# Edge batch norm sums moved to TensorE, degree counts moved to the second edge stage

## The reference

```python
h = jnp.maximum(_layernorm(x), 0.0)
messages = jnp.concatenate([h[src], edge_rep[dst]], axis=-1)
messages = _bn_relu(messages @ W1, g1, b1)      # mean and variance over all 50000 edges
edge_new = segment_sum(messages, dst)
aggregate = segment_sum(edge_new[dst], src)
h = (1.0 + epsilon) * h + aggregate             # then two dense layers with batch norm
```

## Time and profile before

| | us |
|---|---|
| Median of 3 runs | 3554.77 (3550.27 to 3555.87) |
| Profiled execution, first to last instruction | 3565.2 |
| PE busy | 2424.9 (68%) |
| DVE busy | 2395.4 (67%) |
| POOL busy | 1734.6 (49%) |
| ACT busy | 1352.5 (38%) |

### The profile page before, as it was taken

How to read it: one execution, slowest core, us unless ns; L and a number is a source line. 1 busy time by engine, 2 the same in 40 slices (tenths; PEclk the granted TensorE clock), 3 DMA queues, 4 the chain that set the end, 5 groups by cost and what they waited for, 6 DMA issues and landing times. The chain is left out here.

```text
span 3565.2 us, 41686 instructions
## 1 busy us (share of the span) xinstructions
PE 2424.9 (68%) x12339; PEld 1976.6 (55%) x12339; DVE 2395.4 (67%) x4693; ACT 1352.5 (38%) x2800; POOL 1734.6 (49%) x1269
## 2 busy tenths in 40 slices
PE   4668733454555543666621999879999999925998
PEld 3522213454444443444421897469888988923788
DVE  5979945777777778877886544344565566615788
ACT  2268833444444441000000435424434434423776
POOL 0257887776667667888888777730000000042000
PEclk9779865555555555888855999889999999966999
DMA  9993224665555656555533774146545645340355
GB/s 373 351 355 34 22 26 130 174 171 164 165 165 166 172 170 137 133 142 134 143 40 39 202 177 89 1 103 185 175 126 172 185 130 173 118 103 8 109 173 176
DMA packets 338453, 517.84 MB, mean 145 GB/s; under 512 B 145379, under 2 KB 227100, under 8 KB 331580
## 3 DMA queue, kind: packets, MB, share of 16 engines
q1 hardware_dynamic: 190254, 436.41, 38.2%
q0 software_dynamic: 134768, 58.41, 14.2%
q10 hardware_dynamic: 13214, 20.35, 1.7%
HBM read 369.65 MB, written 145.38 MB: 144 GB/s over the span
## 5 line engine op out<-in xcount | busy, mean ns | idle before, releaser
L1133 PE MATMUL banks<-rows_r,lhs_r 128*128 128x448 f32 x3500 | 899.1, 372 | 84.0 <-issue 41.6
L728 POOL DMA_INDIRECT counts<-wts x391 | 637.4, 1630 | 307.9 <-DMA counts<-ring 141.0
L1133 PEld LDWEIGHTS banks<-rows_r,lhs_r 128*128 128x128 f32 x3500 | 667.8, 191 | 152.9 <-issue 74.8
L741 POOL DMA_INDIRECT weights<-wts x391 | 620.9, 1588 | 161.8 <-issue 159.1
L1133 PE MATMUL banks<-ring_r,lhs_r 128*128 128x448 f32 x1750 | 525.8, 370 | 0.0
L749 POOL DMA_INDIRECT reg<-tab_p,w x416 | 406.9, 978 | 217.9 <-issue 122.8
L548 DVE SCALAR_TENSOR_TENSOR ring_r<-ring,dinv,rows_r 128x896 fp32r<-128x896 f32 (+1 forms) x300 | 303.7, 1033 | 309.5 <-ACT rows_r L535 309.3
L1221 PE MATMUL banks<-lhs_r,oT 128*128 x416 | 203.3, 489 | 429.8 <-issue 346.6
L535 ACT ACTIVATE rows_r<-ring,dinv 128x896 fp32r<-128x896 f32 (+1 forms) x300 | 285.0, 951 | 399.3 <-PE banks L1133 342.0
L799 POOL DMA_INDIRECT el<-tab_l,base_i x25 | 24.0, 958 | 796.8 <-DMA tab_l<-reg 789.5
L1221 PEld LDWEIGHTS banks<-lhs_r,oT 128*128 128x128 f32 x416 | 131.9, 317 | 447.3 <-issue 447.0
(11 more groups left out here) (269 smaller groups left out, 4104.6 us busy)
## 6 DMA issues: line engine op xcount, KB each, us to landing
ring<-weights SPq DMA_DIRECT2D x225, 448.0 KB
ring<-counts SPq DMA_DIRECT2D x150, 448.0 KB
zbuf<-reg SPq DMA_DIRECT2D x208, 256.0 KB
reg<-zbuf SPq DMA_DIRECT2D x52, 1024.0 KB
counts<-ring SPq DMA_DIRECT2D x25, 1568.0 KB, 16.4
weights<-ring SPq DMA_DIRECT2D x25, 1568.0 KB
ring<-weights SPq DMA_DIRECT2D x75, 224.0 KB
dr<-low_rows_d SPq DMA_DIRECT2D x52, 256.0 KB
```

The costliest lines, as they stand in the source:

```text
L728: pool.indirect_dma_start(counts, bass.IndirectOffsetOnAxis(ap=ix_c[:, k:k + 1], axis=0), vals_c[:, k:k + 1], None, compute_op=ALU.add).th ...
L741: pool.indirect_dma_start(weights, bass.IndirectOffsetOnAxis(ap=ix_w[:, k:k + 1], axis=0), vals_w[:, k:k + 1], None, compute_op=ALU.add).t ...
L1133: m = pe.matmul(bank[:, 0:BLK], lhs[part], rows[:, c:c + BLK], start=first, stop=last)
```

## The change

ScalarE's squares and VectorE's running sum are gone. TensorE multiplies z with itself: for each chunk and each half of the channels, 128 columns of z against the same 128 columns and two columns of ones beside them. The diagonal of the result is the sum of squares, the ones' column the sum of z. So z lies with gaps between its rows (`ZW`), and the statistics are columns, one channel per partition, instead of rows. The degrees move from the first edge stage to the second, the clearing of `en` from VectorE to ScalarE. Eight tile numbers are loaded by one instruction. GpSimd issues one count after every eighth gather instead of every fourth, and fewer weights between the counts that follow.

```diff
-C_PER = 1
-W_FROM, W_PER, W_MID = 42, 7, (7, 7, 4, 3, 7)
+C_EVERY = 8
+W_FROM, W_PER, W_MID = 42, 7, (4,) * 15 + (3,)
...
+        def load_tiles(eng, regs, i):
+
+            eng.load(regs, tile_ix[0:1, 8 * i:8 * i + 8])
+            return [eng.snap(r, min_val=0, max_val=NT - 1) for r in regs]
...
                 for q in (2 * s, 2 * s + 1):
                     sp.dma_start(zbuf[:, 2 * q:2 * q + 2, :],
-                                 zz[q % ZS].rearrange("p (a c) -> p a c", c=H)).then_inc(z_stored[s % (ZS // 2)], 16)
+                                 z_rows(q)).then_inc(z_stored[s % (ZS // 2)], 16)
...
             for i in range(NPASS):
-                if i == 2:
-                    sp.wait_ge(stat_done, 1)
+                if i == 0:
+                    sp.wait_ge(z_acc, KQ)
...
                 gather(k)
-                if k % 4 == 3:
-                    add_counts(C_PER)
+                if k % C_EVERY == C_EVERY - 1:
+                    add_counts(1)
...
-            for i in range(NPASS):
-                for q in range(4 * i, 4 * i + 4):
-                    act.wait_ge(z_ready, q + 1)
-                    act.activation(zsq[q % SQ], zz[q % ZS], ACT.Square).then_inc(sq_ready, 1)
-                    for c in (2 * q, 2 * q + 1) if i < NBAT else ():
...
+            act.activation(bn_c[:, 3, :], bn_c[:, 2, :], ACT.Sqrt).then_inc(bn_std, 1)
+            for at_t in (en, en_odd):
+                act.activation(at_t, zeros[:, 0:H].unsqueeze(1).to_broadcast([P, NT, H]), ACT.Copy).then_inc(en_cleared, 1)
+            for c in range(NCH):
+                act.activation(dist[c % 2], cols[:, :], ACT.Abs, bias=t_nlo[:, c:c + 1]).then_inc(dist_ready, 1)
...
-                    tiles[2 * q:2 * q + 8] = [pe.value_load(tile_ix[0:1, k:k + 1], min_val=0, max_val=NT - 1) for k in range(2 * q, 2 * q + 8)]
+                    tiles[2 * q:2 * q + 8] = load_tiles(pe, pe_regs, q // 4)
...
+            def square_sums(q):
+
+                pe.wait_ge(z_ready, q + 1)
+                for k in range(2):
+                    for j in range(JH):
+                        o = 2 + k * (H + 2) + j * P
+                        a = o - 2 if j == 0 else o
+                        m = pe.matmul(stat_bank[j][:, 0:P + 2], zz[q % ZS][:, o:o + P], zz[q % ZS][:, a:a + P + 2],
+                                      start=(q == 0 and k == 0), stop=(q == KQ - 1 and k == 1))
+                m.then_inc(z_acc, 1)
...
                     add_q(q)
-                    if i and i <= NBAT:
-                        degrees(2 * q - 8)
-                        degrees(2 * q - 7)
+                    if q >= 2:
+                        square_sums(q - 2)
...
                     m.then_inc(m_sum, 1)
+                    if i < NBAT:
+                        degrees(2 * q)
+                        degrees(2 * q + 1)
...
-                if i < NBAT:
-                    degree_rows(i)
                 for q in range(4 * i, 4 * i + 4):
                     add_z(q)
-                    if q >= 2:
-                        sum_z(q - 2)
...
+                if i + 1 < NBAT:
+                    degree_rows(i + 1)
+                tiles = load_tiles(v, v_regs, i)
```

More of the change, by code:

```diff
@@ L290, in gnn_kernel, with z_rows @@
         low_sb = typed("low_sb", reg_at + 4 * at, 4 * P, BF16); at += 2 * P
[L291 removed]
+        low_sb_end = at
+        assert low_sb_end <= F0 + 44 * H
         gp = view(F0, 8, H)
[L294 to L305 removed]
+        Z_AT = F0 + 16 * H
+        zz = [view(Z_AT + k * ZW, ZW) for k in range(ZS)]
+        def z_rows(q):
+            return view(Z_AT + q % ZS * ZW + 2, 2, H + 2)[:, :, 0:H]
+        at = Z_AT + ZS * ZW
+        dr = [typed(f"dr{k}", reg_at + 4 * at + 2 * k * 8 * P, 8 * P, BF16) for k in range(2)]
+        at += 8 * P
+        oT = [rounded(f"oT{k}", at + k * 8 * P, 8 * P) for k in range(2)]
+        at += 2 * 8 * P
+        assert at <= 6 * W_ - NG * P
         at = F0 + 44 * H
@@ L1210, in _ @@
             tiles = [None] * KS
+            pe_regs = [pe.alloc_register(f"pe_tile{k}") for k in range(8)]
             def add_q(q):
@@ L1243, in _ @@
                     group_totals(TESTED[q])
-            pe.wait_ge(z_acc, KQ + 1)
-            for part in range(2):
-                for k in range(2):
-                    o = (2 * part + k) * H
-                    m = pe.matmul(stat_bank[:, part * H:(part + 1) * H], ones[:, :], zsum[:, o:o + H], start=(k == 0), stop=(k == 1))
-            m.then_inc(stat_done, 1)
-            pe.wait_ge(abs_a, 1)
+            pe.wait_ge(nb_ready, 1)
             for j in range(JH):
-                m = pe.transpose(ps[5][:, j * P:(j + 1) * P], absg[:, j * P:(j + 1) * P], ident[:, :])
-            m.then_inc(a_cols, 1)
+                m = pe.matmul(nb_ps[:, j * P:(j + 1) * P], bn_c[:, 7, j:j + 1].to_broadcast([P, P]), ident[:, :], start=True, stop=True)
+            m.then_inc(nb_rows, 1)
             for i in range(NPASS):
@@ L1662, in _ @@
-            v.wait_ge(a_cols, 1)
-            do(v.tensor_scalar(neg_a[:, :], ps[5][:, 0:H].rearrange("p (j c) -> p j c", j=JH)[:, :, 0], -1.0, None, ALU.mult))
+            v.wait_ge(z_acc, KQ)
+            mean_c, sq_c, var_c, std_c, a_c, ra_c, bt_c, nb_c = (bn_c[:, k, :] for k in range(8))
+            for j in range(JH):
+                o = 2 if j == 0 else 0
+                v.tensor_tensor(diag_t[:, j, :], stat_bank[j][:, o:o + P], ident[:, :], ALU.mult)
+                last = v.tensor_scalar(mean_c[:, j:j + 1], stat_bank[j][:, 0:1] if j == 0 else stat_bank[j][:, P:P + 1], 1.0 / E, None, ALU.mult)
@@ new lines, in _ @@
+            do(last)
+            do(v.tensor_reduce(sq_c, diag_t, AX_X, ALU.add))
+            do(v.tensor_tensor(var_c, mean_c, mean_c, ALU.mult))
+            do(v.scalar_tensor_tensor(var_c, sq_c, 1.0 / E, var_c, ALU.mult, ALU.subtract))
+            do(max_zero(var_c))
+            v.tensor_scalar(var_c, var_c, BN_EPS, None, ALU.add).then_inc(bn_var, 1)
+            do(v.tensor_scalar(bt_c, g_col[:, :], 0.0, None, ALU.is_ge))
+            do(v.tensor_scalar(bt_c, bt_c, 2.0, -1.0, ALU.mult, ALU.add))
@@ L1676, in messages @@
                                 ALU.max).then_inc(msg_ready, 1)
+            v_regs = [v.alloc_register(f"v_tile{k}") for k in range(8)]
             destinations(0)
+            v.wait_ge(nb_rows, 1)
+            do(v.tensor_copy(nb_row[:, :], nb_ps))
             messages(0)
+            v.wait_ge(en_cleared, 2)
+            degree_rows(0)
             for i in range(NPASS):
@@ L1683, in _ @@
                     messages(i + 1)
-                tiles = [v.value_load(tile_ix[0:1, k:k + 1], min_val=0, max_val=NT - 1) for k in range(8 * i, 8 * i + 8)]
+                if i + 1 < NBAT:
+                    degree_rows(i + 1)
+                tiles = load_tiles(v, v_regs, i)
                 for k in range(8 * i, 8 * i + 8):
@@ L1692, in _ @@
             do(v.tensor_tensor(en, en, en_odd, ALU.add))
+            v.wait_ge(deg_done, NCH)
+            do(v.tensor_copy(cnt, deg_bank[:, NT:2 * NT]))
+            do(v.tensor_scalar(dinv[:, :], deg_bank[:, 0:NT], 0.0, None, ALU.is_gt))
+            do(v.tensor_tensor(sc[:, 2, :], deg_bank[:, 0:NT], dinv[:, :], ALU.mult))
+            do(v.tensor_tensor(sc[:, 2, :], sc[:, 2, :], dinv[:, :], ALU.subtract))
+            v.tensor_scalar(sc[:, 0, :], sc[:, 2, :], 1.0, None, ALU.add).then_inc(deg_var, 1)
+            v.wait_ge(deg_std, 1)
+            do(v.reciprocal(sc[:, 2, :], sc[:, 1, :]))
+            do(v.tensor_tensor(dinv[:, :], dinv[:, :], sc[:, 2, :], ALU.mult))
             def pair_tests(i):
```

107 lines of the change are left out of this document (39 added, 68 removed).

## The result

| us | median | runs | ratio to before (95%) |
|---|---|---|---|
| before, beside it | 3553.53 (3550.27 to 3555.87) | 4 | |
| changed kernel | 3594.71 (3590.12 to 3603.01) | 4 | 1.0122 [1.0100, 1.0144] |
| forecast | 3481 (3446 to 3527) | | 0.979 |

The account below looks back on a forecast made before the run. GpSimd's scatter queue bounds the start of the second dense pass. Of the 3565.2 us span: -96 waiting, +20 staying, -1 moved counts, +3 added group, -74, span 3491; median 10.4 us lower, 3481 us, range 3446 to 3527.

Parts of the forecast that it names:

- What is left of the 96 us of waiting: First edge stage: of GpSimd's 96 us of waiting for VectorE, between 0 and 96 stay, 20 taken.
- rival D: First edge stage: VectorE waits for the gathered rows themselves, so 60 of the 96 us stay, 3521 us; chance 0.11.
- one more group of 14 that waits for its predecessors: GpSimd's scatters behind the gathers: the 52 moved counts add one such group, about 3 us.
- Moving them is worth 0 to 4 us: Moving 52 counts behind the gathers: 98 us there against 100 us in the edge stage; 1 us of gain taken.
- GpSimd's pass without waits: First edge stage: 12.15 us a pass with one count, 632 us for 52; 730 us for the kernel before.
- the clock above 0.6: TensorE in the first edge stage: granted clock rises from 0.50 to above 0.6, as the long gaps go.
- the second edge stage: Second edge stage, with the degrees added: 7.4 us a pass, 385 us for 52 passes.
- which path sets the dense pass: Start of the second dense pass: GpSimd's scatters still release it, with TensorE idle 39 us ahead of it.
- that level exists in the first dense pass: DMA share rising from 0.59 to about 0.76: scatters there average 1623 ns, contention at most 36 us, counted within the 20.
- A: GpSimd beats its means: counts fall to 1547 ns, gathers get somewhat quicker, no wait stays; 3446 us, chance 0.15.
- B: TensorE bounds the first edge stage at the half clock, 13.3 us a pass, 42 us come back; 3523 us, chance 0.17.
- C: TensorE at the half clock in both edge stages, its path sets the second dense pass; slower, 3599 us, chance 0.07.

Follow-up runs that it names:

- the lists with good borders: GpSimd's new list with seven-weight groups beginning right behind seven counts: in the changed kernel 1.0027 (old list there 0.9932), alone in the kernel before 1.0078.
- The quarter of the products: Changed kernel without three of the four products of z with itself in every q but the first and last (sums wrong): 3581.28 us, 1.0087.
- the three kernels meant to decide: Changed kernel with GpSimd's old list and, in turn, hardly any products, sixteen more tiny products a pass, eight loads on TensorE: 1.0006, 0.9994, 1.0005.
- the list alone: Kernel before with only GpSimd's list changed: one count a pass instead of two, weights 7, 4, 3, 4, 3, ... behind the gathers: 3591.28 us, 1.0078.

## Why the forecast was wrong

**The step that failed** is "What is left of the 96 us of waiting ... I take 20". 102 us were left, 82 more than that. By the milestones the stage took 725 us where 652 were forecast, 73 of the 101 us between the forecast span of 3491 and the measured 3592.0. (The medians are 114 us apart: the forecast put the median 10 us below the profiled span, and it came out 2.7 above it.) I had asked who is busy when GpSimd waits (VectorE 74%, TensorE's eight loads), and took them for the cause. The same kernel with the same loads and a busier VectorE has no wait at the 3452 us level, so neither is a cause by itself. What the waits end with is a late signal of TensorE; that the load and the sums take away room to catch up behind it fits the 51 us of the single load, but no run shows it by itself. The earlier trace rows held the hint: "remote", 105.5 us, was the largest of VectorE's waits, and I gave it to the gathered rows (rival D). In the trace's records all 28 of those waits end with TensorE's signal for the product. At the other level VectorE waits 159.6 us for gathered rows, and GpSimd does not notice.

**The second step** is "one more group of 14 that waits for its predecessors, about 3 us". The gaps cost 28 us, for I counted groups and did not look at what stands right in front of each border. Behind the gathers the 52 counts, with ten weights moved behind the last count, cost 125 us (104.8 + 20.2) where the forecast had 98 + 3. From the last gather to the last count it took 687 us where 658 were forecast. Those 29 us, with the 73 above and -2 at the start, -1 to the last weight and +2 behind it, are the 101.

The sum between the two traces at the first level: -2.2 at the start, -98.5 in the edge stage (forecast -174), +104.8 to the last count, +20.2 to the last weight, +2.5 to the end: +26.8 us of span. At the other level -102.9 + 107.7 + 20.1, and 3.4 for start and end: +28.3. There the change had nothing to win, since no wait was left. The traces differ by about the same at both levels, the medians do not: 41 us (1.0122) against 24 (1.0070). At the first level a typical run of before is 12 us shorter than the one in the trace, so the change did not only leave the waiting there, it may have added some. The term "Moving them is worth 0 to 4 us" holds at the other level: if the gaps cost 28 us there too, which is an estimate, moving the counts costs nothing. At the first level it costs 28 to 34 us by the ratios of the lists with good borders, because some of the counts between the gathers had filled waits.

**Right:** GpSimd's pass without waits, 632 us for the stage (630.5 measured at the 3452 us level), and 730 us for the kernel before (733.4). The one load of eight numbers, taken as 0.6 us, is this row:
```profile
L567 PEldq TENSOR_LOAD <-tile_ix x52: 587/593/1389, 493.0 to 1258.3; - x52
```
That row agrees with the floor of about 600 ns in the Trainium skill, page "DMA: Bandwidth & Descriptors", section "Latency and other measured facts"; the single number's 301 ns in the earlier trace rows lies under it. Right too: the clock above 0.6 (0.73), the second edge stage (384 us, 7.4 a pass), 425 us from the last count to the last weight (426 forecast), and which path sets the dense pass. Not right, though the sum does not use it: GpSimd "about 83% busy" in the stages after the gathers. In the last of them it is 75% (305.23 of 405.00), at 2.15 us a scatter. And "that level exists in the first dense pass", said of a DMA share of 0.76, does not hold for the stage: the earlier trace rows has 0.52.

**The rivals.** A: the counts' mean stayed at 1616 ns and the gathers' at 979, and the wait stayed. B: the clock rose, no bound; its sum is also wrong, since 11.5 us and the dearer load are 13.3 us a pass already without the 1 us for slow stretches. With it the pass is 14.3 us and the time some 3575 us, not 3523. D: 102 us stayed and not 60, and not for the gathered rows, which came in 3.3 us. C, "slower", came out by its sign but not by its mechanism: its half clock and its pass of 9.5 us are nowhere.

**What stays open:** what makes TensorE's signals and instructions come late, and with it the cause of the 102 us; what puts a job at one level or the other (chip number 7 had both); and whether the number of TensorE's instructions matters at the slower one. The ten traces at the slower level also hold fewer records of semaphore updates than the ten at the other (29771 against 44291 for the kernel before); whether the recording takes part in the waits, no run shows. The quarter of the products and the float32r copies moved the wait by 9 and 13 us, less than I expected, and the three kernels meant to decide ran at the other level. The Trainium skill, page "Perfetto Trace Analysis", section "Summary: the profiler window per engine type", says that TensorE's reported end is an estimate and that the way of a semaphore is hidden. In the example above the row's end and the record of the signal are 7 us apart (1183.02 and 1190.01), in line with it; which of the two is off, nothing here shows.

**The better version:** float32r products with GpSimd's old list. 0.9901 [0.9869, 0.9932] where before takes 3566 us, 1.0000 [0.9990, 1.0010] where it takes 3453. The single load alone gives 0.9933 with a far smaller edit, and the intervals overlap.

## What to carry to other kernels

A wait that ends with a busy engine is not caused by its being busy: ask for each long one what that engine itself waited for, and do not count on a lighter load to remove what the rows call "remote" or "issue". Before work is moved out of a stage whose engine waits, count it at its full price at the new place and at less than its price at the old one (here about 72 of 100 us with the list alone, and the full 103 where nothing waited). When a list with group borders is re-cut, look at what stands right ahead of each border, not at how many borders there are.

## What was not expected of the hardware

The same program ran at 3553 to 3566 us in some jobs and at 3452 to 3454 us in others, with the runs of a job within 0.6% of each other. Between the two traces of before (117.5 us apart) 90 us are the edge stage, and the part behind the last weight is 1209 us at one level and 1186 at the other. TensorE's signals are recorded well behind the ends of their rows (7 us in the example above) at the slower level only. The instruction queue fetched 16 KB some 30 times in the edge stage in about 1 us each at either level, so the fetches themselves aren't slower. Sixteen more float32 matmuls a pass, 2 columns by 2, cost nothing at the faster level.
